# Six of eight normalised tiles transposed by DMA in 16-bit halves, beside a new order of the other operations

## The reference

```
x   = x + tanh(g_x) * (fake_quant(layernorm(x)) @ fake_quant(ctx))        # per batch: 512x1024 @ 1024x1024
h   = layernorm(x)
out = x + tanh(g_f) * (h @ W_base.T + b_base + moe(h))
moe(h): gate = softmax(h @ W_gate.T); thr = sigmoid(h @ W_thr + b_thr) / 8
        w = max(gate - thr, 0), divided by its sum; sum_e w_e * (h @ A_e.T) @ B_e.T * 2      # 8 experts, rank 16
```

## Time and profile before

| | |
|---|---|
| median of three runs | 191.94 us |
| the profiled execution, its own time | 191.66 us |
| span of its instructions | 189.8 us |
| PE busy | 173.8 us (92%) |
| DVE, ACT, POOL busy | 111.5, 78.0, 73.9 us |
| granted TensorE clock | 1.00 |

### The profile page before, as it was taken

One profiled execution on the slowest core, in us unless ns is written; L12 is line 12 of the kernel. 1 busy time (PEld: TensorE's weight loads), 2 busy tenths in 40 slices (PEclk: granted clock), 3 DMA queues, 4 the chain that ended last, 5 costly groups with the idle time before them and its releaser, 6 DMA issues.

```text
span 189.8 us, 2965 instructions
## 1 busy us (share of the span) xinstructions
PE 173.8 (92%) x1093; PEld 151.7 (80%) x1098; DVE 111.5 (59%) x280; ACT 78.0 (41%) x120; POOL 73.9 (39%) x89
## 2 busy tenths in 40 slices
PE   0498999999999997999996999999999999999992
PEld 0483546578899997999952479999999999999992
DVE  1999875989589969925955264564431521521321
ACT  2299814665976396574510116022501410500300
POOL 3470024921001574859798786053500500500400
PEclk9999999999999999999999999999999999999999
DMA  6999999998030037550220000001102002002003
GB/s 222 323 391 389 389 408 407 320 388 315 3 111 3 0 92 241 113 168 2 55 114 0 0 0 0 3 0 45 66 3 111 0 0 114 2 0 111 0 3 111
DMA packets 13694, 23.82 MB, mean 126 GB/s; under 512 B 4967, under 2 KB 6375, under 8 KB 13680
## 3 DMA queue, kind: packets, MB, share of 16 engines
q1 hardware_dynamic: 13666, 23.63, 35.0%
q10 hardware_dynamic: 14, 0.00, 0.0%
HBM read 18.39 MB, written 4.19 MB: 119 GB/s over the span
## 4 chain that ended last, share of the span: by engine, by line
PE 69%; DVE 11%; POOL 7%; ACT 5%; issue 4%; DMA 2%; ACTq 0%; DVEq 0%; POOLq 0%
PE bank L960 14%; PE bank L962 14%; PE bank L961 14%; PE bank L838 9%; POOL colacc L388 6%; DVE st L597 3%; PE bank L948 3%; PE bank L920 2%; PE bank L991 2%; PE bank L896 2%; DMA xs<-in_x_dram 2%; PE bank L985 2%; PE bank L986 2%; PE bank L984 1%; ACT q2u L452 1%
## 5 line engine op out<-in xcount | busy, mean ns | idle before, releaser
L960 PE MATMUL bank<-WTh,lnTh 128*128 128x388 f32 (+1 forms) x192 | 67.5, 351 | 0.0
L962 PE MATMUL bank<-WTh,lnTl 128*128 128x388 f32 (+1 forms) x192 | 65.1, 339 | 0.0
L961 PE MATMUL bank<-WTl,lnTh 128*128 128x388 f32 (+1 forms) x192 | 65.0, 339 | 0.0
L405 POOL TENSOR_TENSOR xs<-xs,tb 128x1024 f32<-128x1024 f32 x8 | 19.3, 2413 | 45.2 <-ACT xs L459 45.2
L960 PEld LDWEIGHTS bank<-WTh,lnTh 128*128 128x128 f32 x192 | 36.2, 188 | 0.6 <-DVE lnTl L655 0.2
L961 PEld LDWEIGHTS bank<-WTl,lnTh 128*128 128x128 f32 x192 | 36.2, 189 | 0.0
L962 PEld LDWEIGHTS bank<-WTh,lnTl 128*128 128x128 f32 x192 | 36.2, 188 | 0.0
L838 PE MATMUL bank<-q,q1T 128*128 128x512 bf16 x123 | 29.7, 379 | 1.1 <-DVE q L627 0.5
L399 POOL TENSOR_TENSOR xs<-xs,colbc 128x512 f32<-128x512 f32 x14 | 18.0, 1315 | 17.1 <-DVE xs L641 12.3
L691 DVE SCALAR_TENSOR_TENSOR xs<-bank,con,xs 128x250 f32<-128x250 f32 (+2 forms) x24 | 13.0, 569 | 19.6 <-PE bank L986 16.0
L838 PEld LDWEIGHTS bank<-q,q1T 128*128 128x128 bf16 x128 | 12.0, 98 | 14.9 <-DVE q1T L585 1.3
(11 more groups left out here) (95 smaller groups left out, 221.3 us busy)
## 6 DMA issues: line engine op xcount, KB each, us to landing
xs<-in_x_dram SPq DMA_DIRECT2D x8, 512.0 KB, 6.9
landing<-in_ctx_dram SPq DMA_DIRECT2D x8, 512.0 KB, 10.9
ring<-in_ctx_dram SPq DMA_DIRECT2D x8, 512.0 KB, 6.3
out_dram<-xs SPq DMA_DIRECT2D x7, 512.0 KB, 2.6
ring<-in_L_ffn_W_base_dram SPq DMA_DIRECT2D x4, 512.0 KB, 13.0
landing<-in_L_ffn_W_base_dram SPq DMA_DIRECT2D x4, 512.0 KB, 15.5
ring<-in_L_ffn_A_w_dram SPq DMA_DIRECT2D x1, 512.0 KB, 11.6
ring<-in_L_ffn_B_w_dram SPq DMA_DIRECT2D x1, 512.0 KB, 4.7
```

Source lines behind the costliest of these rows:

```text
L405: nc.gpsimd.tensor_tensor(xs[:, t, :], xs[:, t, :], tb[:, :], ALU.add).then_inc(xb_ready, 1)
L960: mm(o, hi, WTh[:, k, a:b], start=(k == 0), stop=False, skip_group_check=True)
L961: mm(o, hi, WTl[:, k, a:b], start=False, stop=False, skip_group_check=True)
L962: ins = mm(o, lo, WTh[:, k, a:b], start=False, stop=(k == KT - 1), skip_group_check=True)
```

## The change

Tiles 1, 2, 3, 5, 6 and 7 (`by_dma`) are no longer transposed by PE. ACT takes the f32 tile apart into a plane of low and a plane of high 16-bit halves (`halve`, into `halves` = ring slot 3), a DMA transposes both planes (`transpose_ln`, into `halvesT` = slot 4), ACT joins them again (`join`, into `lnT` = slot 5) and copies the high part (`joined_hi`), and DVE subtracts from SBUF (`joined_lo`). Tiles 0 and 4 keep the old way. Context 8 to 15 has slots 0 to 2 instead of six, so its loads are spread, and some stand behind transposes on SP.

Other operations also move: dummy products (`keep_busy`) before the first tile go from 32 to 48, of which 32 stand ahead of the coefficients; two vector steps before the first `round_q1` change places; the row sums of batch 0 are made tile by tile, in a bank of their own; in iteration 0 of ACT the context precedes the q1 tiles; `round_ctx` 11 and 12 go ahead of the gates of tile 2 on DVE; POOL sums context 10 and 11 one iteration earlier.

The core of the diff:

```diff
+    slots = list(range(NS)) + [0] + [(1, 2, 0)[n % 3] for n in range(CPB)]
+    by_dma = [t for t in range(T) if t % MT]
...
+        elif key == ("rows", 0):
+            i = 2
...
+            def transpose_ln(t):
+                n = by_dma.index(t)
+                if n == 0:
+                    sp.wait_ge(flipped, flip_no["W", 2, 1] + 1)
+                sp.wait_ge(ln_halved, n + 1)
+                if n:
+                    sp.wait_ge(ln_joined, n)
+                sp.dma_start(halvesT, halves, transpose=True).then_inc(ln_transposed[t], 16)
...
+            def halve(t):
+                n = by_dma.index(t)
+                if n == 0:
+                    act.wait_ge(flipped, flip_no["W", 1, 1] + 1)
+                else:
+                    act.wait_ge(ln_transposed[by_dma[n - 1]], 16)
+                act.wait_ge(ln_ready, t + 1)
+                nc.scalar.copy(halves.rearrange("p (h c) -> p h c", h=2),
+                               work[:, t % NW, :].bitcast(U16).rearrange("p (c h) -> p h c", h=2)).then_inc(ln_halved, 1)
+
+            def join(t):
...
+                act.wait_ge(ln_transposed[t], 16)
+                nc.scalar.copy(lnT.bitcast(U16).rearrange("p (c h) -> p h c", h=2),
+                               halvesT.rearrange("p (h k) t -> p h (k t)", h=2)).then_inc(ln_joined, 1)
+
+            def joined_hi(t):
+                act.wait_ge(ln_joined, by_dma.index(t) + 1)
+                if t >= 2:
+                    act.wait_ge(base_part, NP * (t - 1))
+                nc.scalar.copy(lnTh[:, t % 2, :], lnT).then_inc(ln_hi, 1)
...
             normalise(1)
+            halve(1)
             for key in late[7:10]:
                 split_hi(key)
...
+                if t + 1 in by_dma:
+                    join(t + 1)
+                elif t + 1 < T:
                     split_hi(("ln", t + 1, 0))
                     split_hi(("ln", t + 1, 1))
+                if t + 1 == A1_AFTER:
+                    affine_ctx(CPB + 5)
                 split_hi(("hw", t, 0))
+                if t + 1 in by_dma:
+                    joined_hi(t + 1)
...
-                if t + 2 < T and t + 2 != MT:
+                if t + 2 in by_dma:
                     normalise(t + 2)
+                    halve(t + 2)
...
+            def joined_lo(t):
+                dve.wait_ge(ln_hi, by_dma.index(t) + 1)
+                nc.vector.tensor_tensor(lnTl[:, t % 2, :], lnT, lnTh[:, t % 2, :].bitcast(F32),
+                                        ALU.subtract).then_inc(ln_lo, 1)
...
                 split_lo(("hw", t, 0))
+                if t + 1 in by_dma:
+                    joined_lo(t + 1)
...
+            keep_busy(20)
             pe.wait_ge(s_scales, 4 * 16)
...
+            keep_busy(12)
             pe.wait_ge(s_param, 3 * 16)
...
-            keep_busy(32)
+            keep_busy(16)
...
+            row_sums(0, (0, 1))
             flip_q1(3)
-            product_chunk(0, (2, 3))
-            row_sums(0)
-            product_chunk(1, (2, 3))
+            product_chunk(0, (2,))
+            product_chunk(1, (2,))
+            row_sums(0, (2,))
...
-                if t + 1 < T:
+                if t + 1 == MT:
                     flip_ln(t + 1)
```

108 lines of the change are left out of this document (71 added, 37 removed).

## The result

The changed kernel takes 198.23 us (median of four runs, 197.72 to 199.14) against 191.85 us for the kernel before on the same chip: a ratio of 1.0346, 95% interval 1.0326 to 1.0366. It is **slower by 6.4 us**; the forecast was slower by 1.9. The profiled execution took 199.14 us, the slowest of the four and 0.9 us above the median; its span is 197.3 us.

A forecast was written before the change was run, and what follows sets the result against it. PE was taken as the bound, busy 173.8 of 189.8 us. Terms -5.3 - 0.9 + 2.0 + 5.5 - 0.3 - 0.1 + 1.6 + 1.1 - 1.7 gave +1.9 us: 193.6 us, range 190.3 to 198.5.

The forecast's parts named there:

- PE's transposes, -5.3 us: Six tiles' f32 transposes leave PE, each saving 0.88 us: -5.3 us.
- Start, -0.9 us: Ahead of the first column product: row sums fill a wait, moving it from 20.8 to 19.9 us; bounds 0 and -1.3.
- Prices: ACT's `halve` and `join` copies of 2048 16-bit elements: 1.9 us each, bounds 1.0 and 3.8.
- Tile 1, `moe(0)`, +5.5 us: PE waits for `BTl` until 67.5 us, queued behind tile 1's late transpose and `join(1)`: +5.5 us.
- Tiles 2 and 3, +1.6 and +1.1 us less 1.76: Wait at tile 2's gates and hw split +1.6 us, last q1 transpose +1.1, less two tiles' saved PE transposes.
- The last q1 transpose +1.1: Batch 1 products: q1's last transpose lands at 103.0 us, PE's fourth tile is ready at 101.6; net +1.1 us.
- POOL -1.7: Batch 1 products: PE's 1.7 us wait for POOL's column sums goes, since context 10 and 11 are summed earlier.
- Rival 3, the clock: PE falls to its lower clock in the 5.5 us gap at `moe(0)`: +0.8 us, 194.4 us; chance 0.20.
- Rivals 1 and 2: ACT's hand-over copies: cheap at 1.0 us each, 190.9 us, chance 0.28; or doubled at 3.8, 201.5 us, chance 0.12.
- its bounds for clock and landing: Upper end of the range, 198.5 us: the clock and a DMA landing at its upper bound, with part of rival 2.

The follow-up runs named there:

- old start: Start of the kernel before (32 dummy products, old order of vector steps), row sums as changed: in the changed kernel 198.67 us, with only tiles 5, 6, 7 by DMA 186.46.
- order alone: Changed kernel's order with no tile transposed by DMA, PE making all eight tiles' transposes: 189.03 us, 0.9860 of the kernel before.
- dense join: Changed kernel with `join` writing 2048 half words in a row, the high plane twice (output wrong, for timing only): 196.59 us.
- undoing either end: Two runs on the changed kernel: B's splits ahead of `join(1)` and `joined_lo(1)`, 195.16 us; tile 1's transpose ahead of context 10's load on SP, 194.58 us.
- the kernel without tile 1: Changed kernel with tile 1 transposed on PE as before; tiles 2, 3, 5, 6, 7 by DMA: 190.91 us, 0.9953 of the kernel before.
- its roundings filled in: Tiles 2, 3, 5, 6, 7 by DMA, with four roundings moved into DVE's idle time: 189.64 us, from 190.91.
- the queue on SP changed: Tiles 2, 3, 5, 6, 7 by DMA, four roundings in DVE's idle time, q1 tile 4's transpose ahead of tile 3's on SP: 189.00 us.
- the late tiles alone: Changed kernel with only tiles 5, 6 and 7 by DMA, tiles 1 to 3 transposed by PE: 186.99 us, 0.9738 of the kernel before.
- held up at the first gap alone and at both: Changed kernel with 100 dummy products ahead of `moe(0)`, 198.65 us; with 70 more ahead of tile 2's hw transposes, 198.04 us.
- undoing one half of a paired move: Changed kernel with roundings of context 11 and 12 back behind tile 2's gates on DVE, POOL's sums left as changed: 200.53 us.

## Why the prediction was wrong

The sign was right, and so were most of the mechanisms; the size was not: +1.9 us forecast, +6.4 measured.

- **PE's transposes, -5.3 us.** Right for the late tiles: their period is 14.27 us, and three tiles gave 2.0 of 2.65 us in the medians (2.0 in the profiled spans, 187.9 to 185.9; 2.3 by the ratios).
- **Start, -0.9 us.** Wrong: +0.65 in the profile, and between 20.5 and 21.9 us in the 16 profiles with the new start (20.78 before). With the old start and the changed row sums the first column product is at 19.65 to 19.86: the row sums do give the 0.9, and the moved dummy products and vector steps take it back. The forecast took the vector list's work up to the fourth tile as unchanged; PE now waits 1.4 us for the second q1 tile and makes the first transposes and products at 1.2 GHz. In the changed kernel this cost nothing measurable (old start: 198.67), since the landing of tile 1's transpose took up the difference. The order alone still gave the 2.7 us that were forecast for it as 0.9 + 1.7, but not by this term: its first column product is at 20.76, as before. The profiled span shows 1.9 us (189.8 to 187.9), nearly all in the products of batch 1, where PE had waited 1.7 us for POOL; the profiled execution is the slowest of four, 0.8 us above the median, and no trace shows where the others gain this.
- **The sum itself.** It counts the start's 0.9 us, but the times given for PE do not: the second piece of tile 0 at 52.4 is 51.26 + 2.0 - 0.88, and tile 3's first piece at 116.5 is 5.35 us later than before. With three transposes less behind it that is +2.7 us, 194.4: the forecast's own timeline, in the table above, ends 0.8 us above its sum.
- **Prices.** `halve` 1.90, right; `join` 2.53 instead of 1.9. The forecast used one price for a strided read and a strided write, and only the read is free. The rule of the Trainium skill (SBUF — State Buffer, the note on cachelines under the port swizzle), that striding within a line is free, agrees with `halve` and not with `join`; the dense join at 1.90 shows that the writes are the difference.
- **Tile 1, `moe(0)`, +5.5 us.** Right in its chain, from SP's place to `BTl`, and confirmed by undoing either end (moe(0) at 62.1 and at 64.7 us). The wait was 6.2; 0.6 of the join and 0.7 of the landing were under-sized, both within their bounds. As a whole tile 1 cost 7.3 instead of 6.2 us, with the half clock behind its wait in it.
- **Tiles 2 and 3, +1.6 and +1.1 us less 1.76: the failed step.** They cost 3.9 us where the sum had 0.9. The term that was too small is the wait at the gates of tile 2: 1.4 us forecast, 3.6 in the kernel without tile 1; in the changed kernel PE itself comes late, and 2.2 are left. The forecast let the maximum follow ACT's passes at 91.3 us, with two roundings at their usual length: 92.0. It was 3.96 us later. The passes ended at 93.5, since the rounding of q1 tile 4 was at 87.9 instead of 86.6, carried over from tile 1, and the first pass starts only behind it. With roundings of the usual length the maximum would then have been at 94.1 (an estimate: 93.5 and one rounding of 0.6). The other 1.9 us are the roundings' waits for POOL's sums, 1.6 instead of 0.69 us each. The wait of 1.6 us for the landing of the q1 transpose lies beside ACT's passes here and adds little; in the kernel without tile 1 and with its roundings filled in it was 3.0 us, and with the queue on SP changed the maximum moved by 1.8. With the late tiles alone the two roundings are as long (3.23 us for both) and cost nothing, since PE waits no more than 0.6 us there; two tiles fewer on PE, and a chain longer by two copies, find that slack used up. What I missed in the reading is that DVE's list there depends on POOL and on SP, not on ACT alone.
- **The last q1 transpose +1.1, POOL -1.7.** Right in kind, and 0.6 and -1.7 in size.
- **Rival 3, the clock.** It happened, at two gaps instead of one, the second behind a wait of only 2.2 us. The trace agrees with what the Trainium skill says in the place named with this rival (TensorE: Matmul & The Clock Gate, "What's actually happening"): behind both idle times the lower clock was granted. Its price as forecast, 0.8 us, is not refuted: held up at the first gap alone and at both, the clock gave no measurable time, with room for up to 1 us.
- **Rivals 1 and 2** are out: no copy is at half or double price. The range, up to 198.5, held the time, but only just, and by luck: by its bounds for clock and landing and not by what happened at tile 2.

## To carry to other kernels

When work is moved from the bound engine to engines with room on average, cost it tile by tile: here the same hand-over gave 0.7 us a tile where nothing stood behind it, cost 2 us a tile where the first product's work was interleaved, and 7.3 where other operands of PE stood in the queue behind its join. Take it where the queues are slack and leave it where they are full: the late tiles alone were 11 us faster than all six.

Before moving an instruction back, look at what other lists were moved with it. Each list that waits in order passes a delay to work that has nothing to do with it, and undoing one half of a paired move was worse than none.
